# The last five tiles of the second feed-forward layer get their own slots

## The reference

```
x = x + 0.5 * ffn(layernorm(x))
x = x + attn(layernorm(x))
x = x + 0.5 * ffn(layernorm(x))
```

```
scores = einsum('bhqd,bhkd->bhqk', Q, K) / sqrt(D)
thresh = lax.top_k(scores, U)[0][..., -1:]          # U = 31
attn   = softmax(where(scores < thresh, -inf, scores))
context = einsum('bhqk,bhkd->bhqd', attn, V);  out = context @ Wo.T + bo
```

```
rw = gating(hidden)                                  # softmax over the active experts
q = einsum('bte,bted->btd', rw, einsum('btc,ecd->bted', hidden, q_proj))   # k and v alike
attn = einsum('bqk,bkd->bqd', softmax(causal(q k^T / 8)), v)
out  = einsum('bted,edc->btc', attn[:, :, None, :] * rw[..., None], o_proj)
```

## Time and profile before

| what | value |
|---|---|
| median of three runs | 4729.98 us |
| the profiled execution, its own time | 4728.35 us |
| its span | 4726.4 us |
| DVE busy | 4394.2 us (93%) |
| PE, PE weight loads busy | 4139.5 us (88%), 3430.8 us (73%) |
| ACT busy | 3969.8 us (84%) |
| POOL busy | 2995.1 us (63%) |
| DVE busy in 3000 to 4000 us | 981.3 us |
| granted TensorE clock, mean of that stretch | 0.95 |

### The profile page before, as it was taken

One profiled execution on the slowest core, in us unless ns is written; L12 is line 12 of the kernel. 1 busy time (PEld: TensorE's weight loads), 2 busy tenths in 40 slices (PEclk: granted clock), 3 DMA queues, 4 the chain that ended last, 5 costly groups with the idle time before them and its releaser, 6 DMA issues. The chain is left out here.

```text
span 4726.4 us, 123904 instructions
## 1 busy us (share of the span) xinstructions
PE 4139.5 (88%) x33100; PEld 3430.8 (73%) x33100; DVE 4394.2 (93%) x10203; ACT 3969.8 (84%) x10181; POOL 2995.1 (63%) x4946
## 2 busy tenths in 40 slices
PE   6778899899899989999988998899899999987777
PEld 5556777777777777777777777777777777765556
DVE  2499999999999999999999999999999999999982
ACT  2488889899889988889988998899888899888772
POOL 1445677677667766766776776767667777654440
PEclk8888999999999999999999999999999999998888
DMA  3111111111111111111111111111111111110011
GB/s 99 46 27 35 50 51 54 48 55 50 52 51 50 54 49 54 50 54 51 51 53 50 53 50 51 54 49 55 49 53 51 50 53 50 54 38 26 21 30 50
DMA packets 244185, 232.90 MB, mean 49 GB/s; under 512 B 27123, under 2 KB 176628, under 8 KB 243316
## 3 DMA queue, kind: packets, MB, share of 16 engines
q1 hardware_dynamic: 243444, 224.49, 16.5%
HBM read 214.98 MB, written 9.44 MB: 47 GB/s over the span
## 5 line engine op out<-in xcount | busy, mean ns | idle before, releaser
L1027 DVE MAX8 M<-W 128x8 f32<-128x512 f32 x2688 | 1735.6, 681 | 56.0
L679 PE MATMUL pQ<-wf_sb,HS 128*128 128x192 f32 x8192 | 1548.1, 346 | 83.8 <-POOL HS L419 58.1
L679 PEld LDWEIGHTS pQ<-wf_sb,HS 128*128 128x128 f32 x8192 | 1441.1, 203 | 129.3 <-issue 67.2
L1029 DVE MATCH_REPLACE8 W<-M,W 128x512 f32<-128x512 f32 x1664 | 1115.3, 676 | 0.0
L1072 POOL TENSOR_TENSOR XL<-S,LM 128x512 f32<-128x512 f32 x384 | 445.5, 1160 | 913.9 <-ACT LM L909 895.3
L698 PE MATMUL pST<-ident,S 128*128 128x128 f32 x4096 | 749.2, 283 | 13.3 <-ACT S L897 13.3
L924 ACT ACTIVATE OUT<-S,M 128x512 bf16<-128x512 f32 x1024 | 741.7, 724 | 1.1 <-issue 1.1
L928 ACT ACTIVATE S<-S,M 128x512 f32<-128x512 f32 x1024 | 737.1, 720 | 0.0
L700 PE MATMUL pST<-steep,OUT 128*128 128x128 bf16 x4096 | 732.7, 222 | 0.0
L1029 DVE MATCH_REPLACE8 W<-M,S 128x512 f32<-128x512 f32 x1024 | 684.5, 676 | 0.0
L1027 DVE MAX8 M<-S 128x8 f32<-128x512 f32 x1024 | 651.7, 678 | 29.5 <-issue 17.5
(11 more groups left out here) (267 smaller groups left out, 6590.0 us busy)
## 6 DMA issues: line engine op xcount, KB each, us to landing
RB<-rows_b SPq DMA_DIRECT2D x384, 256.0 KB, 3.2
RB<-rows_a SPq DMA_DIRECT2D x384, 256.0 KB, 3.3
x_b<-in_x SPq DMA_DIRECT2D x64, 128.0 KB, 2.8
out_y<-y SPq DMA_DIRECT2D x64, 128.0 KB, 1.8
wf_sb<-in_wf SPq DMA_DIRECT2D x4, 768.0 KB, 7.4
rows_b<-rwT_b SPq DMA_DIRECT2D x64, 8.0 KB, 1.3
wof_sb<-in_wof SPq DMA_DIRECT2D x1, 1024.0 KB, 7.1
rows_a<-rwT_a SPq DMA_DIRECT2D x64, 8.0 KB, 1.4
```

Of the source, the lines that this page charges most:

```text
L679: mm = nc.tensor.matmul(pQ[:, 0:QKV], HS[:, k % 2, e, i, :], wf_sb[:, i, at:at + QKV], start=k + e + i == 0, stop=(k, e, i) == (3, 3, 1))
L1027: nc.vector.max(m, src[i]).then_inc(s_tk, 1)
L1029: nc.vector.match_replace(W[:, i, :], m, src[i], -BIG).then_inc(s_tk, 1)
```

## The change

`LASTS` gives each step of tiles 59 to 63 a slot of its own, relative to the last sequence. All other tiles keep `AT`. `events` puts these slots into the counts on which the waits rest, `slot_of` and `apart` give distances between them, and `hs` is split into `hs0` to `hs3`. Some slots, old and new:

| step | tile 60 | tile 61 | tile 62 | tile 63 |
|---|---|---|---|---|
| `ctx_rec` | 37 to 36 | 53 to 52 | 69 to 66 | 85 to 82 |
| `ctx_norm` | 39 to 36 | 55 to 52 | 71 to 66 | 87 to 82 |
| `x` | 42 to 40 | 58 to 56 | 74 to 72 | 90 to 83 |
| `h` | 46 to 42 | 62 to 58 | 78 to 74 | 94 to 85 |
| `repl` | 53 to 48 | 69 to 62 | 85 to 79 | 101 to 88 |
| `gate` | 55 to 48 | 71 to 62 | 87 to 79 | 103 to 88 |
| `rwT` | 60 to 51 | 76 to 64 | 92 to 81 | 108 to 91 |
| chunks | 64, 66, 68, 70 to 56, 58, 60, 62 | 80 to 86, now 69, 74, 79, 84 | 96 to 102, now 88 to 94 | 112 to 118, now 97 to 103 |
| `y` | 87 to 75 | 103 to 96 | 119 to 104 | 135 to 113 |

Tile 59 keeps its slots up to `qkT` and has the rest earlier (`y` 71 to 67). The store of the gate rows of tile t waited for the `mix` of tile t-2; it now waits for the loads of the rows by that tile, for every tile of both jobs.

```diff
+LASTS = {
+    59: {k: v + 3 * TILE - SPAN for k, v in AT["a"].items()} | {
+        "sc_max": 59, "sc_nmax": 59, "sc_exp": 60, "sc_rec": 60, "sc_norm": 61, "pT": 61, "rb2": 58, "attT": 62,
+        "mix": 63, "y": 67, "out": 68},
+    60: {
+        "ctx_rec": 36, "ctx_norm": 36, "ctxT": 37, "x": 40, "x_mean": 40, "x_sq": 41, "x_rstd": 41, "h": 42,
+        "hT": 42, "h_rinv": 42, "lg": 45, "shift": 45, "top": 47, "pair": 47, "repl": 48, "gate": 48,
+        "gate_exp": 49, "gate_em": 49, "gate_sum": 50, "rw": 50, "rwT": 51, "rw_st": 51, "hs0": 56, "hs1": 58,
+        "hs2": 60, "hs3": 62, "qkv": 64, "qkT": 65, "sc": 68, "sc_max": 68, "sc_nmax": 68, "sc_exp": 69,
+        "sc_rec": 69, "sc_norm": 70, "pT": 70, "rb2": 68, "attT": 71, "mix": 72, "y": 75, "out": 76},
+    61: {
+        "ctx_rec": 52, "ctx_norm": 52, "ctxT": 53, "x": 56, "x_mean": 56, "x_sq": 57, "x_rstd": 57, "h": 58,
+        "hT": 58, "h_rinv": 58, "lg": 60, "shift": 60, "top": 61, "pair": 61, "repl": 62, "gate": 62,
+        "gate_exp": 63, "gate_em": 63, "gate_sum": 64, "rw": 64, "rwT": 64, "rw_st": 65, "hs0": 69, "hs1": 74,
+        "hs2": 79, "hs3": 84, "qkv": 86, "qkT": 87, "sc": 88, "sc_max": 88, "sc_nmax": 88, "sc_exp": 90,
+        "sc_rec": 90, "sc_norm": 91, "pT": 92, "rb2": 88, "attT": 93, "mix": 94, "y": 96, "out": 97},
...
+}
+
+
+def slot_of(n, key, t):
+
+    if n == "a" and t in LASTS:
+        return (NB - 1) * SPAN + LASTS[t][key]
+    return AT[n][key] + t * TILE
...
         def tile(J, key, w, j, ahead=0):
 
-            return due(w, j + ahead, J.at[key], TILE, TILES) if key in J.at else None
+            if w.lo == w.hi and J.n == "a" and key in J.at:
+                for t in LASTS:
+                    if SPAN * w.lo + j + ahead == slot_of("a", key, t):
+                        return t, t - TPB * w.lo
...
                     if not (isinstance(t, int) and t < 2):
-                        held(sp, s_mix, earlier(w, j + J.at["mix"] - J.at["rw_st"] - 2 * TILE, MIXES.values()) + 1)
+                        held(sp, s_rb2, 32 * earlier(w, j + apart(J, t, "rw_st", "mix", 2), MIXES) + 32)
                     sp.dma_start(J.rows[c % 2], J.rwT[:]).then_inc(q["rw_st"], 16)
```

More of the change, by code:

```diff
@@ L72 @@
 }
+LASTS = {
[14 more added lines that the diff above has]
+        "sc_rec": 90, "sc_norm": 91, "pT": 92, "rb2": 88, "attT": 93, "mix": 94, "y": 96, "out": 97},
+    62: {
+        "ctx_rec": 66, "ctx_norm": 66, "ctxT": 69, "x": 72, "x_mean": 72, "x_sq": 73, "x_rstd": 73, "h": 74,
+        "hT": 76, "h_rinv": 75, "lg": 77, "shift": 77, "top": 78, "pair": 78, "repl": 79, "gate": 79,
+        "gate_exp": 80, "gate_em": 80, "gate_sum": 81, "rw": 81, "rwT": 81, "rw_st": 82, "hs0": 88, "hs1": 90,
+        "hs2": 92, "hs3": 94, "qkv": 96, "qkT": 97, "sc": 98, "sc_max": 98, "sc_nmax": 98, "sc_exp": 99,
+        "sc_rec": 99, "sc_norm": 100, "pT": 100, "rb2": 98, "attT": 101, "mix": 102, "y": 104, "out": 105},
+    63: {
+        "ctx_rec": 82, "ctx_norm": 82, "ctxT": 82, "x": 83, "x_mean": 83, "x_sq": 84, "x_rstd": 84, "h": 85,
+        "hT": 85, "h_rinv": 85, "lg": 86, "shift": 86, "top": 87, "pair": 87, "repl": 88, "gate": 88,
+        "gate_exp": 89, "gate_em": 89, "gate_sum": 90, "rw": 90, "rwT": 91, "rw_st": 91, "hs0": 97, "hs1": 99,
+        "hs2": 101, "hs3": 103, "qkv": 105, "qkT": 106, "sc": 107, "sc_max": 107, "sc_nmax": 107, "sc_exp": 108,
+        "sc_rec": 108, "sc_norm": 109, "pT": 109, "rb2": 107, "attT": 110, "mix": 111, "y": 113, "out": 114},
+}
@@ L315, in tile, with apart @@
         def tile(J, key, w, j, ahead=0):
-            return due(w, j + ahead, J.at[key], TILE, TILES) if key in J.at else None
+            if w.lo == w.hi and J.n == "a" and key in J.at:
+                for t in LASTS:
+                    if SPAN * w.lo + j + ahead == slot_of("a", key, t):
+                        return t, t - TPB * w.lo
+            at = due(w, j + ahead, J.at[key], TILE, TILES) if key in J.at else None
+            return None if at and w.lo == w.hi and J.n == "a" and at[0] in LASTS else at
+        def apart(J, t, key, other, back=0):
+            if isinstance(t, int):
+                return slot_of(J.n, other, t - back) - slot_of(J.n, key, t)
+            return J.at[other] - J.at[key] - back * TILE
         def chunk_no(w, j):
-            return earlier(w, j, CHUNKS.values())
+            return earlier(w, j, sum(CHUNKS, []))
         def at_proj(key, w, j):
@@ L432, in layer @@
                 t, c = at
[L433 to L434 removed]
+                n = earlier(w, j, MIXES)
+                eng.wait_ge(q["read"], fill(J.n, w, j + apart(J, t, "mix", "attT")) + 1)
                 eng.wait_ge(s_rb2, 32 * n + 32)
@@ L841, in leave @@
                     t, c = at
-                    wait(act, s_mix, earlier(w, j, MIXES.values()))
+                    wait(act, s_mix, earlier(w, j, MIXES))
                     act.wait_ge(q["full"], n)
```

53 lines of the change are left out of this document (28 added, 25 removed).

## The result

The changed kernel takes 4738.1 us (median of 20 runs, 4735.6 to 4746.2), the kernel before 4729.9 us beside it (20 runs, 4727.3 to 4735.8). The ratio is 1.0021, 95% interval 1.0015 to 1.0027: 8 to 10 us slower, just at the bound of 9.5 us that the prediction set for "no change", and clear of the noise, since the interval leaves 1 out. The profiled execution has a span of 4733.7 us and took 4735.9 us.

The account below looks back on a forecast made before the run. DVE was taken to bound the kernel up to the last selection, a chain of small steps the tail. Span 4726.4 + 19.5 (DVE waits) - 16 (tail) = 4729.9 us, with 1.95 and 1.63 added 4733.5; range 4715 to 4746.

Parts of the forecast that it names:

- the likeliest case: Whole kernel: DVE waits of 14 to 25 us, tail gain 12 to 20; chance 0.43, own range 4723 to 4741.
- no change that can be told: Whole kernel: 3.5 us slower, where about 0.2% (9.5 us) is what a measurement can tell.
- DVE bounds the stretch, the tail bounds the rest: DVE delays move the end until the last selection at 4593.85 us; then 132.4 us are a chain of small steps.
- Part 1: Tile 60's context moved in with DVE's pair 16: queues hold up DVE, pair 20 starts 9.6 us late (5 to 12).
- Part 2: Tile 60's gate in slot 48 on POOL waits for repl: pair 24 starts 1.5 us late (0 to 4).
- Part 3: Tile 61's context moved in with pair 24, x and h earlier: DVE loses 8.4 us (4 to 12).
- Part 4: Tail from pair 28 to the end: 150.2 us against 166.2, so 16 us gained (10 to 24).
- the last choice: Tail length: 152.3 us as worked, 148.5 with the two slow chunks at full clock; 150.2 taken.
- The store's new wait: Store of gate rows waits for loads that were long there in the loop: costs nothing.
- DVE does not wait: Rival: DVE's waits cost 5 us, not 19.5, giving 4719, or none, giving 4714; chance 0.27.
- the tail only trades waits: Rival: late contexts and gate chains cut the tail's gain to 5 us, not 16, giving 4744.5; chance 0.12.
- The lower clock: Rival: PE slow between quad 9's and tile 58's scores, likewise for tile 61; 9 us more, 4742.5; chance 0.15.

Follow-up runs that it names:

- Kernel 6: Kernel 5 with tile 60's gate at POOL's slot 50, not 48, and its gate rows' transpose at 53: 4722.5 us, ratio 0.9969 to 0.9987.
- kernel 1: Changed kernel with tile 60's ctx_rec, ctx_norm, ctxT at slots 37, 38, 38 instead of 36, 36, 37: 4736.9 us, ratio 1.0005 to 1.0023.
- kernel 3: Changed kernel with ctx_norm of tiles 60 and 61 done on DVE, not POOL: 4735.0 us, ratio 1.0000 to 1.0018.
- kernel 5: Changed kernel with tiles 60 and 61's context steps in their old slots, h behind the previous tile's scores, some following steps later: 4720.4 us.
- Kernel 7: Changed kernel with tiles 62 and 63 in their old slots, tile 61's pT, attT, mix one slot later: 4744.9 us, ratio 1.0022 to 1.0045.
- kernel 8: Kernel before with only the gate-row store's new wait, in all 128 tiles: 4731.7 us, ratio 0.9990 to 1.0008.
- kernel 9: Changed kernel with 26 unused extra matmuls on PE ahead of seven waits in the tail: 4726.0 us, ratio 0.9983 to 1.0001.
- kernel 2: Changed kernel with tile 60's h at slot 44, hT and h_rinv at 45, lg and shift at 46: 4738.1 us, ratio 1.0009 to 1.0027.
- kernel 11: Kernel 6 with 29 unused extra matmuls on PE in the tail: 4706.1 us, ratio 0.9937 to 0.9964.

## Why the prediction came out as it did

The time of 4738.1 lies inside the range (4715 to 4746) and the likeliest case's own range (4723 to 4741), 4.6 us above the point. The forecast was "no change that can be told", 3.5 us more; the kernel is slower by 8 to 10 us, on that bound. The net is the small difference of two large terms, and both erred the same way: DVE's waits are 2.1 us more than the sum had, the tail's gain is 4.2 us less, and the gain of 11.8 us lies just under the 12 that the forecast's own case asked for. Step by step:

- **DVE bounds the stretch, the tail bounds the rest.** Right. Kernel 6 takes all of DVE's waits away and the pairs stand where they stood.
- **Part 1, 9.6 us.** Measured 9.76. The stations are right too: `repl` 0.97 us late (1.05), pair 18 3.4 (2.9), the copy of quad 9 18.9 us behind pair 16 (18.5), `sc_max` 6.28 us of wait (about 6.5). The cause as told, instructions that wait in queues in order, is shown by kernels 1, 3 and 5. Two small errors cancelled: quad 9's scores started earlier than worked out (17.7 us behind pair 16, not 18.2), and ACT's copy followed them by 1.2 us, not 0.3. POOL waited 12.61 us before `ctxn`, not 8, because 4.25 us of it stood there before.
- **Part 2, 1.5 us.** Measured 1.95, but the working does not give the 1.5: a copy 10 us later with 6.9 us in hand leaves 3.1. With the contexts put back it is 3.4 us (kernel 5, pair 24 at 71.3 against 67.9). So the near hit is in part luck; that part 1's delay hid some of it in the changed kernel is likely, not shown. Kernel 6 shows that it is the gate's slot.
- **Part 3, 8.4 us.** Measured 9.9. The copy of quad 13 came 20.3 us behind pair 24, not 18.4: to assume part 1's pattern was near, not exact.
- **Part 4, 16 us.** Measured 11.8: this is the term that was mis-sized. The stations up to the last chunk came out within 2 us: quad 12's transposes 25.6 (25.9), gate of tile 62 71.95 (70.1), tile 62's first chunk 95.3 (93.5), the end of the last chunk 132.8 (130.9). Of the 4.2 us that are missing, half had come in by the gate of tile 62, between quad 12's transposes and quad 15's (which end at 68.6, not 66.8). The other half is the last choice: the working with both slow chunks gave 152.3, and I took 150.2, about half-way to the full clock. The run had both slow (4.92 and 4.59 us). Kernel 7 shows that the new slots of tiles 62 and 63 bring about 6.7 us, not all of it as I said.
- **The store's new wait, nothing.** Right (kernel 8).
- **Rivals.** "DVE does not wait" is refuted by the timeline, "the tail only trades waits" by its 11.8 us. "The lower clock" was right in kind and looked for in the wrong place: between quad 9's scores and tile 58's it cost no more than the sum had, while in the tail it was worth 11 us (kernel 9), as much as the slots gained there. Its premise, every burst behind a wait slow, did not hold as such: the chunk behind the context's wait took 4.29 us, but the tail's chunk behind a wait of 1.93 us took 2.87. I had it as a few slow chunks in a sum; I had not asked what filling PE's gaps would give.

## What to carry to other kernels

To move a step earlier in a queue that runs in order is only free where what it waits for is also earlier. Here `ctx_norm` waited for a reciprocal that stands behind DVE's newest pair, and every instruction behind it on POOL and on PE, the bounding engine's own input among them, paid for it; with the same steps behind work that was ready (kernel 5) DVE got 18 of its 21.6 us back for nearly the same tail. And where PE runs short pieces between waits in a latency-bound tail, read the granted clock there first: unused matmuls in the gaps, no longer than the gaps, shortened the tail by 11 to 19 us in three kernels, and by 2.8 us in the fourth, where four of them stood in no gap and cost 3.4 us.

## What the runs showed of the hardware

- The same chunk of 16 matmuls took 2.77 us without a wait at the full clock (2.4 GHz, granted clock 1.00) and 4.25 to 5.49 us, mostly at 1.2 GHz, behind waits of 1.5 to 7 us; the 5.49 us had a granted clock of 0.50 throughout. The same chunk behind a wait of 1.9 us took 2.87 us in the changed kernel and kernel 5, and 4.44 and 5.49 in kernels 2 and 6, so the wait just ahead does not settle it.
- `ctxn`, 128x256, took 0.62 us on POOL and 0.42 to 0.43 us on DVE. But in the kernel before, two of DVE's (at 4594.71 and 4634.75 us) took 2.18 and 2.57 us: both ran beside a product of 1024 columns on POOL and ended 0.3 us behind it, and the second of these products took 2.88 us, not 2.37. In the changed kernel they do not meet. What that gave the tail is not shown.
- A matmul of 512 columns in f32 has two rows in the trace (52 for 26). It took 0.88 to 0.90 us at the full clock (four, 8 rows, in 3.60 us; seven, 14 rows, in 6.28 us in kernel 9 and 6.17 in kernel 11, granted clock 1.00 in each). Four of kernel 11's, behind short pieces and waits near its end, took 5.30 us, where the granted clock was 0.68.
